# A weighted sum moved ahead of both row pairs in the steps of the first attention

## The reference

```python
q, k, v = (proj(Wq), proj(Wk), proj(Wv))
q = _apply_rope(q, cos, sin)
k = _apply_rope(k, cos, sin)
scores = jnp.einsum('bhqd,bhkd->bhqk', q, k) / math.sqrt(hd)
scores = scores + causal[None, None]
probs = jax.nn.softmax(scores, axis=-1)
ctx = jnp.einsum('bhqk,bhkd->bhqd', probs, v)
```

## Time and profile before

| | before |
|---|---|
| median of 3 runs | 2631.1 us (2626.42 to 2639.3) |
| the profiled execution | 2626.75 us, span 2624.8 us |
| PE busy | 2517.0 us (96%) |
| DVE busy | 1837.5 us (70%) |
| ACT busy | 1392.1 us (53%) |

### The profile page before, as it was taken

One profiled execution on the slowest core, in us unless ns is written; L12 is line 12 of the kernel. 1 busy time (PEld: TensorE's weight loads), 2 busy tenths in 40 slices (PEclk: granted clock), 3 DMA queues, 4 the chain that ended last, 5 costly groups with the idle time before them and its releaser, 6 DMA issues. The chain is left out here.

```text
span 2624.8 us, 49577 instructions
## 1 busy us (share of the span) xinstructions
PE 2517.0 (96%) x16744; PEld 2100.9 (80%) x16744; DVE 1837.5 (70%) x4034; ACT 1392.1 (53%) x2454; POOL 401.0 (15%) x305
## 2 busy tenths in 40 slices
PE   6998999899999999998999999999999999999999
PEld 6864454488888888887888888888877788888888
DVE  6677777567777767766777777777777677677673
ACT  4524555655555555545555555555555555555553
POOL 2031000101222122212011011010010321221220
PEclk9998889899999999999999999999999999999999
DMA  4054322000000000000000000000000000000000
GB/s 164 1 148 77 50 28 58 33 1 33 32 0 33 32 0 32 20 0 20 2 21 21 1 20 21 1 20 1 20 33 1 33 33 3 30 32 26 5 1 32
DMA packets 19134, 73.80 MB, mean 28 GB/s; under 512 B 3344, under 2 KB 8208, under 8 KB 15632
## 3 DMA queue, kind: packets, MB, share of 16 engines
q1 hardware_dynamic: 18960, 71.78, 9.7%
HBM read 61.02 MB, written 10.49 MB: 27 GB/s over the span
## 5 line engine op out<-in xcount | busy, mean ns | idle before, releaser
L372 PEld LDWEIGHTS ps<-w,hid 128*128 128x128 f32 x5376 | 699.2, 190 | 57.1 <-DVE rb L453 13.6
L372 PE MATMUL ps<-w,hid 128*128 128x256 f32 x5376 | 719.5, 283 | 1.8 <-DVE rb L453 1.5
L337 PE MATMUL ps<-xT,w 128*128 (+1 forms) x2688 | 705.3, 398 | 10.0 <-DVE xT L522 10.0
L530 DVE TENSOR_TENSOR hid<-gel,hid 128x512 fp32r<-128x512 f32 x448 | 397.0, 896 | 341.1 <-ACT hid L413 333.1
L407 ACT ACTIVATE gel<-ps,b 128x512 f32<-128x512 f32 x448 | 307.3, 686 | 550.1 <-issue 542.7
L337 PEld LDWEIGHTS ps<-xT,w 128*128 128x128 f32 x2688 | 479.0, 190 | 88.9 <-issue 10.3
L413 ACT ACTIVATE hid<-gel 128x512 fp32r<-128x512 f32 x448 | 272.4, 620 | 0.0
L905 PE MATMUL ps<-pT,v_sb 128*128 128x512 f32 (+3 forms) x1152 | 260.8, 357 | 1.6 <-DVE pT L1029 1.6
L879 PE MATMUL ps<-k_sb,q_sb 128*128 128x512 f32 (+3 forms) x1152 | 253.4, 353 | 3.7 <-ACT p_lo L971 2.3
L1018 DVE TENSOR_REDUCE negmax<-ps 128x1 f32<-128x128 f32 (+7 forms) x256 | 192.4, 752 | 77.7 <-PE ps L882 76.3
L1559 DVE TENSOR_REDUCE nmx<-ps 128x1 f32<-128x512 f32 (+3 forms) x384 | 196.1, 553 | 68.1 <-PE ps L1342 40.4
(11 more groups left out here) (139 smaller groups left out, 2909.8 us busy)
## 6 DMA issues: line engine op xcount, KB each, us to landing
wraw<-in_wffn SPq DMA_DIRECT2D x12, 2048.0 KB, 8.2
wraw<-in_w_a SPq DMA_DIRECT2D x8, 1280.0 KB, 5.5
qk_dram<-rope_hl SPq DMA_DIRECT2D x16, 512.0 KB, 3.1
xT<-qk_dram SPq DMA_DIRECT2D x48, 128.0 KB, 5.5
x<-in_x SPq DMA_DIRECT2D x4, 512.0 KB, 8.1
xb<-in_wffn SPq DMA_DIRECT2D x2, 1024.0 KB, 7.1
rot<-in_rot SPq DMA_DIRECT2D x1, 2048.0 KB, 15.6
xb<-in_wffn SPq DMA_DIRECT2D x1, 2048.0 KB, 14.9
```

The source lines that it names most:

```text
L337: last = nc.tensor.matmul(ps[:, HPS + j % 4, :], w[par][:, wp, 0, k * HIDDEN + j * PART:k * HIDDEN + (j + 1) * PART], xT[:, xp, k, bass.ds ...
L372: last = nc.tensor.matmul(y_ps[:, t, :], hid[:, hp, j % 4, t * PART:(t + 1) * PART], w[par][:, wp, 1, j * DIM:(j + 1) * DIM], start=j == 0 ...
L530: nc.vector.tensor_tensor(hid[:, 1, j % 4, :], gel[:, j % 4, :], hid[:, 0, j % 4, :].bitcast(f32), ALU.subtract).then_inc(low_done, 1)
```

## The change

`rows_beside(i, 0)`, which puts a step's first row pair into the plan, is called later: behind the weighted sum (and X) and right ahead of the second row pair. Nothing else changes; each engine has the same instructions, and the banks of the ring go to the same items.

```diff
                 if i < steps:
                     todo += [("T", i // len(TILE_STEPS), i % len(TILE_STEPS), p) for p in range(2)]
-                rows_beside(i, 0)
                 if i >= AV_LAG:
                     g, s = divmod(i - AV_LAG, len(TILE_STEPS))
                     todo.append(("A", g, s))
...
+                rows_beside(i, 0)
                 rows_beside(i, 1)
                 todo += late.pop(i, [])
```

## The result

The changed kernel takes 2711.9 us (median of 4 runs, 2689.5 to 2724.8), the kernel before 2628.8 (4 runs): ratio 1.030, interval 1.022 to 1.038. It is slower by 83 us; 2683 was forecast, with 2650 to 2735 as the range.

What follows compares the result with a forecast made beforehand. PE was taken to bound the 80 steps with row pairs. New waits of 63.6 us, less 18.9 and 2.7, gave 42; with +10 for the clock, +52 us, so 2683 us, range 2650 to 2735.

Steps and rivals of the forecast that it cites:

- What bounds the stage: The 80 steps with row pairs: PE is the engine to follow, and a longer step lengthens the kernel.
- The delay between adjacent pairs: Start to start of two row pairs: start of reduction, first reduction and handover, 1.35 us at 512 columns.
- What the change adds and takes away: PE's waits in the 80 steps: 63.6 us added, 18.9 and 2.7 us removed, net 42 us.
- The step check: Steps s = 7 and 8 worked out whole: +0.38 and +0.64 us, mean 0.51, times 80 is 41 us.
- The parts at nothing: A's wait for exponentials, X, normalising of C, DMA, last 16 steps, change of array form: no term of their own.
- The clock: Granted clock in the stage falls more often with a wait in every step: +10 us taken.
- the signs of being wrong: Second pairs find banks free, A waits for ScalarE, or clock in slices 4 to 8 below 0.75 or at 1.
- the first rival: "The clock gives way": 42 + 90 us and more, given as 2740 to 2790 us; chance 0.10.
- The clock gives way: Rival: the stage stays mostly at the low clock, 2740 to 2790 us; chance 0.10.
- Hidden anyway: Rival: clock stays up (-15 us) and T, A, U cost less in the new order, +13 us or less; chance 0.08.
- faster: Rival: second pairs find their banks free, the 18.9 us of waits go and nothing comes, 2610 us; chance 0.04.
- slower, by less: Rival: clock falls less often than now, or hidden tails are larger, +13 to +25 us; chance 0.08.

Runs made afterwards that it cites:

- e1: Changed kernel with both row pairs still side by side but ahead of A (order T, pair, pair, A): 2730.4 us, ratio 1.036.
- e2: Changed kernel with the second row pair moved between the two halves of the next step's T: 2672.6 us, ratio 1.017.
- e4: Changed kernel with VectorE's maximum taken over only the first half of each row pair's columns: 2701.1 us, ratio 1.026.
- e3: Changed kernel with one to three useless zero-weight matmuls, by pair width, added between a step's two row pairs: 2656.7 us, ratio 1.010.
- f3: Kernel before with one or two useless matmuls ahead of row pairs in s = 8, 9 and 10 of each group: 2617.8 us, ratio 0.9943.
- f4: Changed kernel with a single useless matmul of 512 columns between a step's two row pairs: 2671.1 us, ratio 1.013.

## Why the prediction was right, and where it was off

**What bounds the stage: right.** PE's time there is the kernel's time; outside the stage nothing moved by more than noise.

**The delay between adjacent pairs: right.** 1.35 us was forecast at 512 columns and 1.36 measured in the steps shown (1.35 to 1.45 in all those at the upper clock), 1.06 and 1.07 at 256. e1, e2 and e4 vary what stands around it, between it and inside it, and it answers as the sum of its three parts: only a shorter reduction (e4) shortens it. It is not the same at either clock, as the prediction had it ("1.35 us in all steps of 512 columns"): at the lower level it is 1.67, since the time from the pair to its first reduction grows. A ring with a fourth bank, which would test the cause from the other side, was not tried.

**What the change adds and takes away: right in size.** 63.6 us of new waiting were worked out; the trace counts 59.8 us, one of its 81 waits lying ahead of the first step. An idle row begins at the modelled end of the pair ahead (0.50 us at 512 columns) and not where the next work could begin (0.43), which is the difference. First pairs wait no longer. The net of 42 us measures 37.7 us at the upper clock (e3 against f3). The step check, 41 us, erred the same way: s = 8 was put at 3.52 and measured 3.38 us, with T at 0.68 and not 0.77 and A at 0.57 and not 0.64. The stage's end, put near 509, came at 543.7; that is the clock's part.

**The parts at nothing: right.** A never waited for ScalarE in the changed kernel; PE's only wait in the stage is the one shown.

**The clock: right in sign, mis-sized.** This is the term that failed: I took +10 us, and it is 88.1 - 37.7 = 50 us in the profiled run. Two of its factors were off. I took a third of the stage as low, and it was about 183 of 327 us, 0.56. And I took a low stretch to lose 0.27 of itself, by carrying over the absolute loss of two old steps; it loses (9.94 - 6.27) / 9.94 = 0.37. In the old steps PE idled less when the clock was low (0.29 us of 7.55 and not 0.63 of 5.08), which took off part of the loss; with nothing between the pairs the idle time stays, 1.48 us in two steps at either level. With these, 183 x 0.37 = 68 us, less the 15.6 of before, gives 52. The share could not be read from the trace of before, which had a low start and five short falls. Its low stretches in mid-stage, of 3 to 10 us, grew to as much as 44; that they last because a low stretch has the wait in each step too is my reading, and no run shows it.

**Within the range partly by luck.** The sum was 31 us short of the change measured, 52 against 83. It stayed in the range because the upper end allowed 45 us for the clock, a bound chosen and not worked out. Of the signs of being wrong that the prediction named, one came: the clock in slices 4 to 8 is 0.73, below its 0.75. Its numbers also disagree in two places: +25 to +95 us is not the range of 2650 to 2735, which is +19 to +104, and the first rival's 42 + 90 gives some 2763, where 2740 stands as its lower end.

**The rivals.** "The clock gives way" came half true: the stage was low for more than half of its time, not for nearly all, and the total stayed below the 2740 us given for it. "Hidden anyway", "faster" and "slower, by less" fell to the measured waits and the lower clock. The rule of the Trainium skill on cycling through PSUM banks (TensorE: Matmul & The Clock Gate, A second HAM failure mode) agrees with these traces: waits of 0.9 us at most, in each step, and a clock at 0.72. The Trainium skill's rule that a change of tiling mode drains TensorE (TensorEngine Tiling, Key Properties) is tested by no run here: e1 too keeps the count of changes at two a step, and the cost of a single one was not measured.

**Left open.** How the clock's low time varies from run to run (2689 to 2725 us for the same program) was seen and not explained, and what exactly begins or ends a low stretch was not found.

## What to carry to other kernels

Before work is put side by side, count the banks: with a ring of three and two banks a unit, the next unit's start is tied to the first reduction of the one ahead, and what stood between two units may be a cover and not a delay. Price the uncovered wait per step from start, reduction and handover in the trace, and the clock as a second term, which here cost more than the wait. Where PE must wait, harmless matmuls in the gap can be worth having: they took 55 us off the changed kernel (e3) and 15 off the kernel before (f3).

## What the runs showed of the hardware that I had not expected

- With idle gaps of no more than 0.9 us, one in each step, the granted clock was at half for up to 44 us at a time, while PE counted as busy for 268 of 327 us. With fillers in the gaps it did not fall (e3).
- Matmuls with zero weights help to hold the clock: with them it stayed at the upper level from 241.0 us to the end of the stage at 484.7 (e3), at no cost in step length (s = 8: 3.37 us with, 3.38 without).
- One filler of 0.21 us a step was enough to hold a clock that was up for 223 us (f4), though PE still idled for 32 of them. The low start of the stage took 30 us without fillers, 27 with three and 60 with one; what sets it was not found.
- Half the clock did not take half of the speed: two steps of the changed kernel went from 6.27 to 9.94 us, with PE's busy time from 4.79 to 8.46 and its idle time unchanged at 1.48.
